# A two-layer recurrent and attention model on one core: order of the first layer's activations, attention output split to f16 halves in its own stage, earlier loads for the output stage

## The reference

```python
xn = layernorm(x)
s  = rwkv_attention(xn)          # r, k, v from xn mixed with the previous token; a scan over time; @ Wo
g  = silu(relu(xn @ W1 + b1) @ W2 + b2)                  # 256 -> 1024 -> 256
x  = x + s * g
xn = layernorm(x)
s  = softmax(clip(Q K^T, -80, 80) / sqrt(24), causal) V @ W_O   # 16 heads of 16, latent projections, rotary part of 8
g  = silu(sigmoid(xr @ W_r) * (relu(xk @ W_k)**2 @ W_v))
x  = x + s * g
```

## Time and profile before

| what | us |
|---|---|
| median of 3 runs | 2026.55 |
| the profiled execution | 2026.82 |
| its span (first to last instruction) | 2025.1 |
| stage 1, layer0 | 0 to 638 |
| stage 2, projections | 638 to 952 |
| stage 3, attention | 952 to 1960.8 |
| stage 4, output | 1960.8 to 2025.1 |
| TensorE busy over the span | 1900.1 (94%) |
| VectorE, ScalarE, GpSimd busy | 1729.8, 1727.0, 547.4 |

### The profile page before, as it was taken

The page is one execution under the profiler, slowest core; times in us unless marked ns, Lnnn a source line. Parts: engine busy times, 40 slices in busy tenths (PEclk is TensorE's granted clock), DMA queues, the critical chain, the costliest instruction groups (busy, mean ns, idle before and its releaser), DMA issues. The chain is left out here.

```text
span 2025.1 us, 53401 instructions
## 1 busy us (share of the span) xinstructions
PE 1900.1 (94%) x22950; PEld 978.9 (48%) x22950; DVE 1729.8 (85%) x2249; ACT 1727.0 (85%) x2153; POOL 547.4 (27%) x426
## 2 busy tenths in 40 slices
PE   3999999999995999998999999999999999999986
PEld 1565565655653566664444443444434444344445
DVE  5999999999987788886888888888888888888878
ACT  5767867777666888886999999999999999999972
POOL 0564554655644666764000000000000000000004
PEclk9999999999997999998999999999999999999999
DMA  3001001001112356567221222222222222122129
GB/s 108 22 22 42 22 22 42 22 22 42 54 42 78 129 191 204 190 170 210 70 75 55 67 68 74 73 55 68 68 74 72 62 62 55 51 62 60 56 96 329
DMA packets 130220, 166.24 MB, mean 82 GB/s; under 512 B 13632, under 2 KB 101696, under 8 KB 129728
## 3 DMA queue, kind: packets, MB, share of 16 engines
q1 hardware_dynamic: 127952, 160.59, 26.5%
q10 hardware_dynamic: 2032, 2.24, 0.3%
HBM read 91.21 MB, written 71.57 MB: 80 GB/s over the span
## 5 line engine op out<-in xcount | busy, mean ns | idle before, releaser
L1757 ACT ACTIVATE c_probs<-c_ps_b 128x1536 f32<-128x1536 f32 x544 | 891.9, 1640 | 0.0
L1871 PE MATMUL c_ps_o<-c_probs,c_v 128*32 128x256 f32 (+3 forms) x6656 | 582.3, 453 | 3.9 <-DVE c_probs L1789 0.8
L1789 DVE TENSOR_SCALAR c_probs<-c_probs 128x2048 f32<-128x2048 f32 (+2 forms) x415 | 433.7, 1055 | 68.2 <-ACT c_probs L1757 67.8
L1851 PE MATMUL c_ps_b<-c_qk 24*128 24x256 f16 (+2 forms) x8064 | 459.9, 294 | 5.7 <-PEq L1094 5.7
L1851 PE MATMUL c_ps_a<-c_qk 24*128 24x256 f16 (+2 forms) x2688 | 449.9, 294 | 6.5 <-ACT c_probs L1756 4.9
L1756 ACT ACTIVATE c_probs<-c_ps_a 128x512 f32<-128x512 f32 x544 | 422.9, 777 | 2.5 <-PE c_ps_a L1851 2.4
L1851 PEld LDWEIGHTS c_ps_b<-c_qk 24*128 24x128 f16 x8064 | 222.8, 93 | 332.6 <-ACT c_probs L1757 243.9
L2022 POOL TENSOR_TENSOR d_prod<-d_prod,d_x 128x1024 f32<-128x1024 f32 x4 | 13.1, 3262 | 1029.4 <-DVE d_prod L2011 1029.4
L1871 PEld LDWEIGHTS c_ps_o<-c_probs,c_v 128*32 128x32 f32 x6656 | 161.7, 109 | 245.8 <-issue 126.9
L278 POOL TENSOR_TENSOR a_hidh<-a_hid,a_hidh 128x512 f16<-128x512 f32 x128 | 207.2, 1648 | 135.2 <-ACT a_hidh L404 134.0
L1794 DVE TENSOR_SCALAR c_probs<-c_probs 128x1536 f32<-128x1536 f32 (+2 forms) x208 | 165.6, 803 | 55.9 <-ACT c_probs L1757 53.6
(11 more groups left out here) (272 smaller groups left out, 2776.9 us busy)
## 6 DMA issues: line engine op xcount, KB each, us to landing
v_d<-b_val SPq DMA_DIRECT2D x16, 1024.0 KB
c_v<-v_d SPq DMA_DIRECT2D x64, 256.0 KB
rows<-in_x SPq DMA_DIRECT2D x16, 512.0 KB, 4.9
x_d<-rows_out SPq DMA_DIRECT2D x16, 512.0 KB, 3.3
rows<-x_d SPq DMA_DIRECT2D x16, 512.0 KB, 5.0
qc_d<-b_qc SPq DMA_DIRECT2D x16, 512.0 KB
kc_d<-b_kc SPq DMA_DIRECT2D x16, 512.0 KB
gate_d<-rows_out SPq DMA_DIRECT2D x16, 512.0 KB, 3.3
```

The source lines that it names most:

```text
L1757: nc.scalar.activation(probs[:, t % NPROB, PARTS[1]], ps_b[:, t % 2], ACT.Exp, scale=unscale).then_inc(exp_b_done, 1)
L1789: nc.vector.tensor_scalar(tile, tile, P_MAX, P_MIN, ALU.min, ALU.max).then_inc(clip_done, 1)
L1851: mm = nc.tensor.matmul(into, k[rows, hk, kt * P:(kt + 1) * P], tokens[rows, hq], start=(i == 0), stop=(i == len(TERMS) - 1), tile_positio ...
L1871: mm = nc.tensor.matmul(ps_o[j * VW:(j + 1) * VW, column:column + w], v[:, kt, j * VW:(j + 1) * VW], probs[:, step % NPROB, j, at:at + w], ...
```

## The change

In stage 1, ScalarE's relus and exponentials alternate strictly; `normalise` of a chunk is issued one chunk earlier, at the end of ScalarE's body; and of VectorE's two `mixed_low` subtractions the values' one is issued in the next body, behind L696. In stage 3, the transposed output is scaled and split into f16 halves by two new VectorE instructions, `high` and `low`, one and two steps behind the transpose; the DRAM tensor of the attention rows holds the halves side by side (the same number of bytes); the stores wait for `low` and stand two steps later; and in the last group SyncE loads the attention rows of 6 chunks and x1 of 4 more, one DMA in every second step, partly into operand memory that has become free. In stage 4, ScalarE's and VectorE's splitting is gone, TensorE waits for the load itself, and there are 12 slots for loads.

```diff
@@ layer0, scalar engine
                     if following:
-                        normalise(n + 1, c + 1)
                         xn_of(n + 1, c + 1)
-                    hidden(n, 0)
-                    exponential(n, 0)
-                    exponential(n, 1)
-                    hidden(n, 1)
-                    exponential(n, 2)
+                    for m in range(3):
+                        hidden(n, m)
+                        exponential(n, m)
 
                     highs = 0
                     for m in range(2, MT):
                         if first and m == MT // 2:
                             act.wait_ge(w_low, 5)
-                        hidden(n, m)
+                        if m > 2:
+                            hidden(n, m)
...
                 act.wait_ge(scale_done, 2)
+                normalise(1, 1)
                 for i in (3, 4, 5):
                     weight_high(i)
...
                 mixed_high(1)
+                normalise(2, 2)
...
                     if left >= 2:
                         mixed_high(n + 2)
+                    if left >= 3:
+                        normalise(n + 3, c + 3)
@@ layer0, vector engine
                     nc.vector.tensor_tensor(rwkv_half[:, 1], rwkv[:], rwkv_half[:, 0], ALU.subtract).then_inc(rwkv_low, 1)
+                    if left >= 1:
+                        mixed_low(n + 1, 1)
...
                         mix(n + 2)
-                        mixed_low(n + 2)
+                        mixed_low(n + 2, 0)
@@ scratch
-        "attn": dram("attn_d", [DIM, TOKENS]),
+        "attn": dram("attn_d", [DIM, 2 * TOKENS], F16),
@@ attention, sync engine
-                    sp.wait_ge(ot_done, e + 1)
+                    sp.wait_ge(ot_low, e + 1)
...
-                for t in range(N + LAG + 5):
-                    if t - LAG - 4 in end_at:
-                        store(end_at[t - LAG - 4])
+                for t in range(N + LAG + 7):
+                    if t - LAG - 6 in end_at:
+                        store(end_at[t - LAG - 6])
...
-                    if group == BATCH * GROUPS - 1 and 0 <= part < ahead.ROWS:
+                    if group == BATCH * GROUPS - 1 and part % 2 == 0 and 0 <= part // 2 < 2 * ahead.SLOTS - 2 - ahead.ROWS:
                         if part == 0:
-                            for o in range(OUTS):
-                                sp.wait_ge(stored[o], 16 * GH * (GROUPS * CPB // OUTS) + 16 * GH)
-                        sp.dma_start(ahead.attn[:, part], channel_view(d["attn"])[part]).then_inc(ahead.loaded[part], 16)
+                            sp.wait_ge(pv_done, group * STEPS)
+                        i = part // 2
+                        if i < ahead.ROWS + 2:
+                            if i % CPB == 0:
+                                for o in range(OUTS):
+                                    sp.wait_ge(stored[o], 16 * GH * ((i // CPB + 1) * GROUPS * CPB // OUTS) + 16 * GH)
+                            sp.dma_start(ahead.attn(i), channel_view(d["attn"])[i]).then_inc(ahead.loaded[i], 16)
+                        else:
+                            sp.dma_start(ahead.x1(i - 2), token_view(d["x1"])[i - 2]).then_inc(ahead.loaded[i - 2], 16)
@@ attention, vector engine
+                def high(e):
+
+                    dve.wait_ge(ot_done, e + 1)
                     dve.wait_ge(stored[e % OUTS], 16 * GH * (e // OUTS) + 16 * GH)
+                    nc.vector.tensor_scalar(o_half[:, e % OUTS, :, 0, :], o_norm[:].rearrange("p (n t) -> p n t", t=HALF), scales.attn[:], None,
+                                            ALU.mult).then_inc(ot_high, 1)
+
+                def low(e):
+
+                    dve.wait_ge(ot_high, e + 1)
+                    nc.vector.scalar_tensor_tensor(o_half[:, e % OUTS, :, 1, :], o_norm[:].rearrange("p (n t) -> p n t", t=HALF), scales.attn[:],
+                                                   o_half[:, e % OUTS, :, 0, :], ALU.mult, ALU.subtract).then_inc(ot_low, 1)
...
-                for t in range(N + LAG + 3):
-                    for after, task in ((0, reciprocal), (1, normalise), (2, to_channels)):
+                for t in range(N + LAG + 5):
+                    for after, task in ((0, reciprocal), (1, normalise), (2, to_channels), (3, high), (4, low)):
@@ layer1_output
-        SLOTS, ROWS, X_ROWS = ahead.SLOTS, ahead.ROWS, ahead.X_ROWS
-        OUT, HALVES, SUMS = 6, 4, 4
+        ROWS, X_ROWS, MORE = ahead.ROWS, ahead.X_ROWS, 4
+        SLOTS = ahead.SLOTS + MORE
+        OUT, SUMS = 6, 4
...
-                for s in range(X_ROWS, SLOTS):
-                    sp.dma_start(x1(s), x1_v[s]).then_inc(loaded[s], 16)
-                for s in range(ahead.OUTS):
-                    sp.wait_ge(ahead.o_stored[s], batch_stored(SLOTS // CPB))
-                for s in range(ROWS, SLOTS):
+                for s in range(ROWS + 2, SLOTS):
                     sp.dma_start(attn(s), attn_v[s]).then_inc(loaded[s], 16)
+                    if s >= ahead.SLOTS:
+                        sp.dma_start(x1(s), x1_v[s]).then_inc(loaded[s], 16)
...
                 for n in range(NCH):
-                    pe.wait_ge(t_low, n + 1)
+                    pe.wait_ge(*rows_loaded(n))
...
-            @block.scalar
-            def _(act):
...
-                    nc.scalar.activation(attn_t[:, n % HALVES, 0], attn(n % SLOTS), ACT.Copy, scale=attn_scale).then_inc(t_high, 1)
...
-                low(0)
-                low(1)
                 for n in range(NCH):
-                    if n + 2 < NCH:
-                        low(n + 2)
                     dve.wait_ge(out_mm, n + 1)
```

More of the change, by code:

```diff
@@ L1584, in channel_view, with attention @@
 def channel_view(t):
-    return t.rearrange("(k p) (n t) -> n p k t", p=P, t=CH)
+    return t.rearrange("(k p) (n x) -> n p k x", p=P, x=2 * CH)
 def token_view(t):
     return t.rearrange("(n j p) c -> n p j c", j=TPC, p=P)
-def attention(nc, d, rows_out, score_scale, first, ahead):
+def attention(nc, d, rows_out, scales, first, ahead):
     HALF = CH // 2
@@ L1680, in attention @@
         recip = sb("c_recip", [P, 2, BLOCKS])
-        o_norm, stored = ahead.o_norm, ahead.o_stored
+        o_norm = sb("c_onorm", [P, CH])
+        o_half, stored = ahead.o_half, ahead.o_stored
         ps_a = ctx.enter_context(nc.psum_tensor("c_ps_a", [P, 1, CH], F32))
@@ L1695, in attention @@
         ot_done = sem("c_ot_done")
+        ot_high = sem("c_ot_high")
+        ot_low = sem("c_ot_low")
         with nc.Block() as block:
@@ L1750, in _ @@
                 unscale = act.alloc_register("c_unscale")
-                act.load(unscale, score_scale[0:1, 0:1].bitcast(I32))
+                act.load(unscale, scales.score[0:1, 0:1].bitcast(I32))
                 for t in range(N):
@@ L1888, with __init__, sb @@
     OUTS = 4
-    def __init__(self, ctx, nc):
-        def sb(name, shape):
-            return ctx.enter_context(nc.sbuf_tensor(name, shape, F32))
+    def __init__(self, ctx, nc, first):
+        def sb(name, shape, dt=F32):
+            return ctx.enter_context(nc.sbuf_tensor(name, shape, dt))
         def sem(name):
@@ L1897, in __init__, with attn, x1, layer1_output @@
         self.gate = sb("d_gate", [P, NCH, TPC, DIM])
-        self.attn = sb("d_attn", [P, self.ROWS, KT, CH])
-        self.o_norm = sb("c_onorm", [P, self.OUTS, CH])
+        self.attn_rows = sb("d_attn", [P, self.ROWS, KT, 2 * CH], F16)
+        self.o_half = sb("c_ohalf", [P, self.OUTS, 2, 2, CH // 2], F16)
         self.o_stored = [sem(f"c_stored{i}") for i in range(self.OUTS)]
-        self.x1 = sb("d_x1", [P, self.X_ROWS, TPC, DIM])
+        self.x1_rows = sb("d_x1", [P, self.X_ROWS, TPC, DIM])
+        self.first = first
         self.gate_loaded = sem("d_gate_loaded")
         self.loaded = [sem(f"d_loaded{i}") for i in range(self.SLOTS)]
-def layer1_output(nc, d, scales, ahead, out):
+    def attn(self, s):
+        if s < self.ROWS:
+            return self.attn_rows[:, s]
+        return self.first.memory[:, 1, s - self.ROWS].rearrange("p (k x) -> p k x", k=KT)
+    def x1(self, s):
+        if s < self.X_ROWS:
+            return self.x1_rows[:, s]
+        s -= self.X_ROWS
+        if s < 2:
+            return self.first.v[:, KEYT // 2 * s:KEYT // 2 * (s + 1)].rearrange("p m e -> p (m e)").rearrange("p (j c) -> p j c", j=TPC)
+        return self.first.memory[:, 0, s - 2].bitcast(F32).rearrange("p (j c) -> p j c", j=TPC)
+def layer1_output(nc, d, rows_out, scales, ahead, out):
     with ExitStack() as ctx:
@@ L1913, in sem @@
             return ctx.enter_context(nc.semaphore(name))
-        SLOTS, ROWS, X_ROWS = ahead.SLOTS, ahead.ROWS, ahead.X_ROWS
-        OUT, HALVES, SUMS = 6, 4, 4
+        ROWS, X_ROWS, MORE = ahead.ROWS, ahead.X_ROWS, 4
+        SLOTS = ahead.SLOTS + MORE
+        OUT, SUMS = 6, 4
         LOADS = 16 * 2
         early_rows = 16 * (TPC - 1)
-        w_o, gate, loaded = scales.w_o, ahead.gate, ahead.loaded
-        more_attn = sb("d_more_attn", [P, SLOTS - ROWS, KT, CH])
```

(15 more changed lines are left out.)

49 lines of the change are left out of this document (23 added, 26 removed).

## The result

The changed kernel takes **2000.16 us** (median; 2000.06 to 2001.22) where the kernel before takes 2026.93 (2025.97 to 2027.44): ratio 0.9871, 95% interval 0.9857 to 0.9885, **26.8 us faster**. The forecast was 2002.5 in a range of 1998 to 2012.5. The profiled execution took 2001.22 us, its span is 1999.5.

The account below looks back on a forecast made before the run. Bounds: two nearly equal loops in stage 1 (TensorE's and the rwkv loop), ScalarE in stage 3, DMA in stage 4. Stage 1 16.1, start -0.8, stage 4 9.0: 24.3 off 2026.82 gives 2002.5 us, range 1998 to 2012.5.

Parts of the forecast that it names:

- Stage 1's two loops: Stage 1: TensorE's loop 35.67 us a chunk, the rwkv loop beside it 35.5; period taken as 35.7, 16.1 us gained.
- (a): Stage 1: `normalise` moved into ScalarE's idle time lets transposes start right behind the keys, 0.46 us less a chunk.
- (b): Stage 1, relu order: 0.8 of TensorE's 1.0 us wait in the hidden products stays, moved from product 3 to product 5.
- (c): Stage 1: one `mixed_low` behind L696 costs its plain 1.2 us; L693 starts 31.8 after out instead of 33.15.
- The start: Start of stage 1: `normalise(1, 1)` ahead of the weight splits shifts ScalarE by 2.06 us; 0.8 us charged.
- Rival B: Stage 1's second loop closes again: period 36.4, stage gain 4.8, time 2012.7 us; chance 0.27.
- Stage 3: Stage 3: `high` and `low` add 91 us to VectorE's idle time, nothing on the path; 1.4 us after the last transpose.
- Rival D: Stage 3: `high` and `low` make VectorE the bound once a clip is over 3 us late; 2047 us, chance 0.03.
- Stage 4: Stage 4 takes 53.8 us, ending 9.0 us earlier; chunk 10 is multiplied at 35.8, 3 us late, behind a store.
- TensorE's slow start: Stage 4: 1.35 us added to TensorE's 43.3 us for a mixed clock after idle time.
- Rival C: Stage 4 stays at DMA speed, held by its six result slots: gain 5 instead of 9, 2006 us; chance 0.16.
- Sum: Whole kernel: 16.1 - 0.8 + 9.0 = 24.3 us off the profiled 2026.82, giving 2002.5 us.

Follow-up runs that it names:

- experiment 9: Changed kernel with third exponential behind sixth relu, stage 4's last loads three stores later, both mixed low halves behind L699, first early normalisation inside first chunk: 2000.83 us.
- experiment 2: Changed kernel with the two exponentials and the relus of the first three hidden products back in the old order: 2002.21 us.
- experiment 3: Changed kernel with the second `mixed_low` of VectorE moved back directly behind the first: 2016.49 us, ratio 0.9949 to the kernel before.
- two of my experiments: Changed kernel with the fourth relu ahead of the first high half: 2003.59 us; the same with both mixed low halves behind L699: 2003.56 us.
- experiment 8: Changed kernel with VectorE computing each low half of the attention three more times into a spare tile: 2059.67 us.
- experiment 7: Changed kernel with the loads of stage 4's last four chunks issued three stores later: 1996.95 us.
- the last two edits together: Changed kernel with the fourth relu ahead of the first high half and both mixed low halves behind L699: 2003.56 us.
- experiment 1: Kernel before with only the first layer changed: 2010.43 us; with only the attention split and stage 4's four more slots: 2015.81 us.

## Why the prediction was right

The mechanism held and not only the number: each sign that it named is in the trace, and undoing its parts one at a time gives nearly the prices that it set. That the third limit of stage 1, which it did not know of, stayed below the other two was luck.

**Stage 1's two loops.** Right. The forecast gave 35.7 a chunk and it is 35.59; the wait before transposes and out went, the relus' 0.8 stayed at the fifth product (0.81). The 0.1 of difference is rounding up of 35.67 and some 0.02 each in keys, values and receptance. L696 starts 31.73 after out, predicted 31.8.

**(a)** The 0.46 of the normalisation was really worth 0.35 when undone alone; the early place also has a price that the prediction did not name: it stands ahead of the high half of the rwkv product. In the changed kernel ScalarE idles 1.00 us there, so it costs nothing; in experiment 9 it costs 1.0.

**(b)** Right to the tenth: 0.2 of 1.0 (experiment 2).

**(c)** Right, and it decides: 0.98 a chunk (experiment 3).

**The start**: charged at 0.8, measured 1.2; but the four profiles with exactly this stage 1 show their first gate product from 82.8 to 83.7, and the two with the old one 81.7 and 82.2, so the term is known to within a microsecond or so only.

**Rival B** (36.4, chance 0.27) had its mechanism right, and experiment 3 is nearly that case. The margin of 0.15 was about 0.2 in truth. What the prediction missed is that a third loop, over GpSimd's low halves, stood some 0.3 to 0.4 under; it cost nothing here, and made two of my experiments fail.

**Stage 3.** Right: nothing on the path. Each new instruction was bounded by 0.71; they take 0.49 and 0.75, so the second is over its bound by 0.04. On the path after the last transpose 1.4 was predicted and 1.27 measured. Rival D's 0.03 is borne out by experiment 8: 140 us more of VectorE's work made the attention only 53 longer. Its threshold was put as a clip's delay; the run shows that the sum of idle time predicts it nearly as well (140 added less 96 idle is 44).

**Stage 4.** 53.8 predicted, 53.7 measured; last add 49.9 in, predicted 49.9; chunk 10 is multiplied 35.5 in behind the late store of chunk 4, predicted 35.8, but the waits begin at chunk 8. To hit the tenth is luck: TensorE's slow start was put at 1.35 and is 2.1, with VectorE held by the stores either way. Rival C's fear, that stores hold the stage, was half right: they cost the 2.9 us that experiment 7 gets back, with the same bytes moved at a higher pace.

**Sum.** Predicted 24.3 off the profiled time, measured 25.6: 1.1 in stage 1 and 0.2 behind it.

## What to carry over

When several loops of nearly one length run through the same engines, undo or add edits one at a time and look which wait appears next: of three edits of this change one decided, and an edit aimed at the visible wait alone made the kernel slower. Work moved into an engine's idle time costs nothing only as long as that idle time stays where it is, so the fit has to be read again after each further edit. For an engine off the path the idle sum was enough for an estimate: 44 us of lengthening by the sums, 53 measured.

## What the runs showed of the hardware that was not expected

**The way into stage 2 is 2 us longer or shorter by the clock.** From the sixteenth gate product to the attention five of the fourteen profiles show 321.0 to 321.7 us and nine 319.2 to 319.9, though the code of stage 2 is the same in all. Most of the difference lies before stage 2's first matmul, in the last "out" of stage 1. In the changed kernel, and in the kernel with stages 3 and 4 changed alone:

```profile
614.49 4.33 PE L733 MATMUL a_ps<-a_wo,a_rwkvh 128*128 128x256 f16 x24 [2.51 <-DVE a_rwkvh L699]
```

```profile
631.32 2.79 PE L728 MATMUL a_ps<-a_wo,a_rwkvh 128*128 128x256 f16 x24 [2.51 <-DVE a_rwkvh L696]
```

The same 24 matmuls behind the same 2.51 us of idle time take 4.33 or 2.79. The granted clock is 0.63 from 614.5 to 618.5, a mix of 0.50 (1.2 GHz) and 1.00 (2.4 GHz), and 1.00 from 631.3 to 635.3. The five long profiles all have the slow one (4.33 to 4.45). The rest of the difference is the rise of the clock later on. TensorE idles 10.2 us before the first projections of stage 2 (640.83 in the changed kernel), waiting for VectorE. Stretches of 4 us, 26 us after the sixteenth gate product, in the same two kernels (columns as in the earlier trace rows):

```profile
640.50:644.50 4.00, 3.67 (x9) 1.34 (x10) 3.95 (x6) 2.20 (x3) 0.01 (x1) 0.50 0.00 0
644.50:648.50 4.00, 4.00 (x16) 1.58 (x14) 1.43 (x2) 2.83 (x6) 4.00 (x2) 0.78 0.02 4
```

```profile
657.30:661.30 4.00, 4.00 (x13) 1.52 (x12) 2.43 (x3) 3.73 (x6) 1.53 (x1) 0.63 0.02 4
661.30:665.30 4.00, 4.00 (x20) 1.54 (x18) 1.73 (x3) 2.34 (x4) 4.00 (x2) 1.00 0.00 0
```

In the first the granted clock is 0.50 and then a mix of both levels; in the second it is at 1.00 a stretch earlier, and 13 and 20 matmuls are done instead of 9 and 16. One profile, of the last two edits together, has a slow last out (4.04) with an early rise, and 319.9. This goes with the half of experiment 1 that gained 10.9 and not 9.2. It may also be why the changed kernel's profiled execution, one with the slow out, took 2001.22 us and its three others 2000.06 to 2000.22, but those three have no kept trace. The Trainium skill, page "TensorE: Matmul & The Clock Gate", Part 1, says that the number of matmuls at the low clock varies from run to run of one kernel; the rows agree as far as kernels with the same stage 2 can show it. No experiment here settled what decides between the two, so some 2 us between two kernels may have nothing to do with their edits.

**Records of ScalarE overlap.** In stage 3 the two exponentials of a step are recorded with 1.64 and 0.78 us on average, 2.42 together, in steps of 1000.0 / 543 = 1.84 us. With ScalarE waiting for TensorE (experiment 8) they shrink to 1.50 and 0.63. So the durations can't be summed to a price there; the prediction took the step, and that held. VectorE's records overlap too, by less (experiment 8).
